# A contiguous copy of each unit's v as the moving operand of the sums over columns

## The chip, the cores and the metric

The kernel runs on one core of a Trainium2 chip. Its time is the device time of one execution in microseconds (us). A comparison of two kernels uses the median of several runs of each on the same chip. A core has five engines that work side by side: PE (TensorE, matrix products), DVE (VectorE), ACT (ScalarE), POOL (GpSimd) and SP (SyncE, which here only issues DMAs). Each goes through its own list of instructions in order and waits at semaphores for the others. Data is held in SBUF, 128 partitions wide; products are summed in PSUM, eight banks of 512 float32 numbers per partition.

## What is computed

A gated block of a sequence model on images: 8 images of 64 x 64 tokens with 96 channels. Each token's vector is divided by its root mean square, and projected to u and v of 288 channels each, with silu. v is then convolved, channel by channel, along the rows and along the columns of the image (`tno`), each with a kernel that a small network computes from the positions. The two results are added, multiplied by u, projected back to 96 channels, and added to x.

```python
xn = srms(x)
u = silu(xn @ u_w.T + u_b)
v = silu(xn @ v_w.T + v_b)
v = v.reshape(b, H, W, NH, HD).transpose(0, 3, 1, 2, 4)
out = (tno(v, -3, rpe2...) + tno(v, -2, rpe1...))
out = out.transpose(0, 2, 3, 1, 4).reshape(b, H, W, NH * HD)
return (u * out) @ o_w.T + o_b + x
```

The convolution of length 64 along one axis is a product with a 64 x 64 Toeplitz matrix for each channel, and two of them fit on 128 partitions.

## The kernel before

The images are worked on in two halves of four. v of one half lies whole in SBUF as `v`, 128 partitions x 128 columns m x 288 channels in float32 (147,456 bytes on each partition). The channel is the innermost index, so one channel's 128 columns lie 288 numbers, or 1152 bytes, apart. u goes to DRAM (`u_dram`) and comes back in tiles `u_in[0..3]` of 4608 bytes.

The program has five stages. **A**: the projection of half 0 in 32 steps, with the position networks beside its first ones. **C0**: the convolution of half 0. **B0**: 32 steps, each with the gate, output projection and store of half 0 and the projection of half 1. **C1**: the convolution of half 1. **B1**: gate, output projection and store of half 1.

A stage C treats the 288 channels as 36 units of 8. For unit n:

- DVE writes two Toeplitz tiles, `toepA` for the columns and `toepB` for the rows (line 749: each in two copies of 64 partitions x 512 numbers, from a `stage` tile that SP loads from `a_dram` by two DMAs, L271). In `stage` a channel's numbers lie 8 numbers (32 bytes) apart. Each Toeplitz tile has two buffers, `stage` three. The quarters that stay zero are written once by POOL (`zero`).
- PE does `along_columns(n)` (L951): 8 float32 products that sum over a column, with `toepA` held still and a channel of `v` moving. The profile has two records for each product, 16 a unit.
- PE does `transpose_v(n+1)` (L934): 8 transposes of v, evacuated by ACT to `vt` (L536).
- PE does `along_rows(n)` (L964): 8 products, again 16 records, that add into the same PSUM banks, with `vt` held still and `toepB` moving.
- ACT copies the sum back into `v` (L542, `evacuate_y`).

`toepA(n+2)` may be written when the columns of unit n are done (`columns_done`), `toepB(n+2)` when its rows are done (`conv_done`). The stage tile of unit n is loaded when both Toeplitz tiles of unit n-3 are written. In C0 DVE also computes the norms of half 1, in 8 groups of 4 steps: SP loads x into `x_n` (L236), POOL squares it (L403), DVE sums it (L655) and takes the root in 14 small operations (4 a unit). The next `x_n` is loaded when that sum is done. In C1 there is nothing of this.

The buffers in SBUF are placed by hand in one region above `v`; many share bytes at different times, and each such pair has a wait. `stage` shares bytes with `u_in`; `x_e` (the x that is added at the end) is loaded by L253 and stored by L259. Every order of instructions is written out by hand in the code.

Of the kernel before, what the change touches and what calls it, by code (L numbers as in the profile page):

```python
# [33 lines left out]
D = 288  # L34
RPE, LAYERS = 256, 3
EPS = 1e-8
P = 128
H = P // 2
# [18 lines left out]
def tno_kernel(nc, x, x_eT, u_wT, u_b, v_wT, v_b, o_wT, o_b, pos_w, pos_b, lwT, lb, out_wT, out_b, out):  # L57
# [7 lines left out]
    with ctx:  # L65
# [21 lines left out]
        XHL = [22528, 28160]  # L87
# [3 lines left out]
        u_out = place("u_out", [P, NB, D], V + 32256)  # L91
        g = place("g", [KE, 2, NCH, TOK], V + 36864, f32r)
        g1 = [place(f"g1{k}", [KE, 2, NCH, TOK], V + 26624 + 12288 * k, f32r) for k in range(2)]
        x_n = place("x_n", [P, CH * NB, E], V + 18432)
# [17 lines left out]
        r_pw = place("r_pw", [P, 2, 2, RC], V + 32256)  # L112
        r_lb = place("r_lb", [P, 2, LAYERS, RC], V + 32288)
# [8 lines left out]
        assert base + K + 8672 <= nc.sbuf_usable_end  # L122

# [41 lines left out]
        vt_transposed, vt_ready = sem("vt_transposed"), sem("vt_ready")  # L165
# [27 lines left out]
        def _(sp):  # L193
# [80 lines left out]
            def after_networks():  # L274
                store_a()
                sp.wait_ge(a_stored, 32)
                load_stage(0, 0)
                load_stage(0, 1)

            def phase_a(c, first, last):  # L280
                if c + 3 < CHUNKS:
                    load_x_all(c + 3)
                for r in range(CH):
                    store_u(0, CH * c + r, u_in[:, r % 2], ua_stored[r % 2])
# [5 lines left out]
            def phase_c(half):  # L290
                if half == 0:
                    sp.wait_ge(ua_stored[1], 16 * (STEPS // 2))
                    load_norms(0)
                load_stage(half, 2)
                for n in range(STAGES, UNITS):
                    load_stage(half, n)
                    if half == 0 and n % 4 == 2 and n // 4 < CHUNKS:
                        load_norms(n // 4)
                    if n == 24:
                        if half == 0:  # L300
                            sp.wait_ge(ua_stored[0], 16 * (STEPS // 2))
                            load_xa(0, 0)
                            load_xa(1, 1)
                        else:
                            sp.wait_ge(ub_stored, 16 * STEPS)
                        load_u(half, 0, 0)
                if half:
                    for k in range(2):
                        sp.wait_ge(o_stored[0][k], 16 * (STEPS // 2))
                else:  # L310
                    sp.wait_ge(norms_summed, 2 * CHUNKS)
                for k in range((2, CH)[half]):
                    load_xe(half, k, k)
                for k in (2, 3, 1):
                    n = UNITS - STAGES + (2, 3, 1).index(k)
# [749 lines left out]
```

## Time and profile before

| what | us |
|---|---|
| median of 3 runs | 985.4 (981.99 to 985.67) |
| the profiled execution | 985.56, of which the span of the trace is 983.8 |
| stage A | 0 to about 179 |
| stage C0 | about 179 to 404 |
| stage B0 | about 404 to 631 |
| stage C1 | about 631 to 859 |
| stage B1 | about 859 to 984 |
| PE busy | 928.7 (94%) |
| DVE busy | 522.7 (53%) |
| ACT busy | 445.2 (45%) |
| POOL busy | 280.6 (29%) |

The trace is one execution. All times in it are counted from its span's start, and 1.8 us of the execution lie outside the span. The busy shares are means over stages that have different limits. PE's granted clock was 0.987 of full speed over the run.

### The profile page before, as it was taken

The numbers are of one execution on the slowest core, as the hardware profiler recorded it, in microseconds if no ns is written. First come the engines' busy times: TensorE is split into PE (matmuls) and PEld (weight loads), VectorE is DVE, ScalarE is ACT, GpSimd is POOL, SyncE is SP. The second block draws the span as 40 slices with busy tenths as digits, with TensorE's granted clock in tenths as the row PEclk, the third lists the DMA queues.
The fourth block names the chain that finished last, engine by engine and source line by source line (L and its number), as shares of the span: only waits on it lengthen the run. The fifth ranks groups of instructions, "written<-read, shape, count | busy, mean of one in ns | idle before, by whom it ended". The sixth has DMA issues, their size and how long they took to land.

```text
span 983.8 us, 17099 instructions
## 1 busy us (share of the span) xinstructions
PE 928.7 (94%) x6124; PEld 855.6 (87%) x6124; DVE 522.7 (53%) x918; ACT 445.2 (45%) x658; POOL 280.6 (29%) x191
## 2 busy tenths in 40 slices
PE   1999689999999999899999999899999999999888
PEld 1998589899999999889898989799999999877665
DVE  7665342486777774344444444444444444277665
ACT  1665467433333333466666666433333333244333
POOL 4332222111111120345454545100000000187664
PEclk9999889999999999999999999899999999999999
DMA  8554643665556553287878777553333434277785
GB/s 200 159 177 153 115 165 145 169 138 121 118 118 159 118 118 107 70 252 254 251 253 251 256 249 249 165 128 86 87 86 86 111 86 110 80 226 249 242 250 188
DMA packets 128871, 160.95 MB, mean 164 GB/s; under 512 B 67174, under 2 KB 93994, under 8 KB 128810
## 3 DMA queue, kind: packets, MB, share of 16 engines
q1 hardware_dynamic: 128810, 160.12, 57.8%
q8 instruction: 40, 0.66, 0.3%
q14 instruction: 21, 0.17, 0.1%
HBM read 109.46 MB, written 50.63 MB: 163 GB/s over the span
## 4 chain that ended last, share of the span: by engine, by line
PE 83%; DMA 10%; DVE 2%; SPq 1%; issue 1%; POOL 1%; ACT 1%; POOLq 0%; ACTq 0%; DVEq 0%
PE ps L951 25%; PE ps L888 20%; PE ps L964 13%; PE ps L908 9%; PE ps L934 6%; DMA out<-x_e 6%; PE ps L898 6%; PE ps L879 3%; DMA u_dram<-u_in 1%; DMA stage<-a_dram 1%; DMA a_dram<-r_a 1%; POOL u_in L456 1%; DMA x_all<-in_x 1%; PE ps L862 1%; DMA u_in<-u_dram 1%
## 5 line engine op out<-in xcount | busy, mean ns | idle before, releaser
L951 PE MATMUL ps<-v,toepA 128*128 128x128 f32 x1152 | 264.8, 396 | 4.4 <-DVE toepA L749 4.4
L456 POOL TENSOR_TENSOR u_in<-u_in,v 128x1152 f32<-128x1152 f32 (+2 forms) x66 | 170.8, 2592 | 294.8 <-ACT v L542 263.0
L951 PEld LDWEIGHTS ps<-v,toepA 128*128 128x128 f32 x1152 | 230.1, 206 | 18.0 <-issue 3.3
L536 ACT COPY vt<-ps 128x1024 f32<-128x1024 f32 x72 | 72.9, 1013 | 244.3 <-PE ps L934 244.3
L749 DVE COPY toepA<-stage 64x512 f32<-64x512 f32 x144 | 106.0, 736 | 132.1 <-PE ps L951 114.3
L908 PE MATMUL ps<-g,wo 96*96 96x512 f32 (+1 forms) x576 | 151.8, 399 | 0.0
L790 DVE TENSOR_TENSOR g<-ps,g 96x512 fp32r<-96x512 f32 x192 | 123.0, 680 | 43.0 <-ACT g L516 43.0
L964 PE MATMUL ps<-toepB,vt 128*128 128x128 f32 x1152 | 140.5, 275 | 0.0
L702 DVE TENSOR_TENSOR xl<-ps,xh 96x512 fp32r<-96x512 f32 x64 | 43.9, 686 | 180.0 <-ACT xh L497 180.0
L964 PEld LDWEIGHTS ps<-toepB,vt 128*128 128x128 f32 x1152 | 134.9, 192 | 0.0
L516 ACT CAST g<-ps 96x512 fp32r<-96x512 f32 x192 | 102.4, 586 | 68.7 <-PE ps L898 68.7
L888 PE MATMUL ps<-wv,xh 97*128 97x288 f32 x512 | 119.8, 309 | 12.4 <-ACT u_in L502 12.0
L749 DVE COPY toepB<-stage 64x512 f32<-64x512 f32 x144 | 96.2, 668 | 57.0 <-PE ps L964 51.4
L888 PE MATMUL ps<-wu,xh 97*128 97x288 f32 x512 | 123.9, 307 | 2.4
L908 PEld LDWEIGHTS ps<-g,wo 96*96 96x96 f32 (+1 forms) x576 | 89.7, 162 | 27.1
L898 PE MATMUL ps<-ident,u_in 128*96 128x128 f32 x768 | 100.1, 273 | 11.0 <-POOL u_in L456 10.8
L898 PEld LDWEIGHTS ps<-ident,u_in 128*96 128x96 f32 x768 | 85.4, 126 | 20.8 <-POOL u_in L456 8.6
L542 ACT COPY v<-ps 128x1024 f32<-128x1024 f32 x72 | 72.9, 1012 | 59.7 <-PE ps L964 59.7
L502 ACT ACTIVATE v<-ps 128x576 f32 (+1 forms) x128 | 83.5, 652 | 35.8 <-PE ps L888 23.8
L888 PEld LDWEIGHTS ps<-wv,xh 97*128 97x128 f32 x512 | 88.0, 192 | 13.4 <-ACT u_in L502 12.3
L888 PEld LDWEIGHTS ps<-wu,xh 97*128 97x128 f32 x512 | 89.2, 190 | 11.2 <-issue 3.9
L934 PEld LDWEIGHTS ps<-ident,v 128*128 128x128 f32 x576 | 77.0, 191 | 3.2
(66 smaller groups left out, 830.1 us busy)
## 6 DMA issues: line engine op xcount, KB each, us to landing
stage<-a_dram SPq DMA_DIRECT2D x144, 256.0 KB, 4.2
u_in<-u_dram SPq DMA_DIRECT2D x64, 576.0 KB, 5.3
u_dram<-u_in SPq DMA_DIRECT2D x32, 576.0 KB, 2.8
u_dram<-u_out SPq DMA_DIRECT2D x32, 576.0 KB, 3.3
x_e<-in_x_eT SPq DMA_DIRECT2D x64, 192.0 KB, 3.9
out<-x_e SPq DMA_DIRECT2D x64, 192.0 KB, 3.5
x_all<-in_x SPq DMA_DIRECT2D x16, 384.0 KB, 5.4
x_n<-in_x SPq DMA_DIRECT2D x16, 384.0 KB, 6.0
```

The source lines that it names most:

```text
L456: return nc.gpsimd.tensor_tensor(out=tile, in0=tile, in1=v[:, bass.ds(t * NB, NB), start:end], op=ALU.mult)
L502: nc.scalar.activation(target, ps[:, b:b + 2, 0:D], ACT.Silu).then_inc(silu_done, 1)
L516: nc.scalar.copy(tile[0:E, 0, k], ps[0:E, bank]).then_inc(gh_ready, 1)
L536: nc.scalar.copy(vt[n % 2][:], ps[:, VT_BANK:VT_BANK + 2].rearrange("p b (c m) -> p (b c) m", m=P)).then_inc(vt_ready, 1)
L749: nc.vector.tensor_copy((toepA, toepB)[axis][n % 2][rows, :, rows], stage[n % STAGES][rows, axis].rearrange("p k c -> p c k")[:, :, ::-1]) ...
L790: nc.vector.tensor_tensor(out=tile[0:E, 1, k], in0=ps[0:E, bank], in1=tile[0:E, 0, k].bitcast(f32), op=ALU.subtract).then_inc(gl_ready, 1)
L888: last = nc.tensor.matmul(ps[:, n, 0:D], (xh, xl)[xp][r % 2][:, n * P:(n + 1) * P], w[:, wp], start=(k == 0), stop=(k == len(SPLIT) - 1))
L898: last = nc.tensor.transpose(columns[:, n // 2, n % 2], u_in[:, r % CH, n, k * E:(k + 1) * E], ident[:])
L908: last = nc.tensor.matmul(ps[0:E, bank], wo[0:rows, wp, k], tile[0:rows, gp, k], start=(k + s == 0), stop=(k == NCH - 1 and s == len(SPLIT ...
L934: last = nc.tensor.transpose(ps[:, VT_BANK + c // NB, (c % NB) * P:(c % NB + 1) * P], v[:, :, UNIT * n + c], ident[:])
L951: last = nc.tensor.matmul(ps[:, SET_BANK[n % 2] + c // NB, (c % NB) * P:(c % NB + 1) * P], toepA[n % 2][:, c], v[:, :, UNIT * n + c], star ...
L964: last = nc.tensor.matmul(ps[:, SET_BANK[n % 2] + c // NB, (c % NB) * P:(c % NB + 1) * P], vt[n % 2][:, c], toepB[n % 2][:, c], start=Fals ...
```

## The change

ACT makes a copy of unit n of v with the channel outermost, so that each channel's 128 columns lie side by side: `vc` (`by_channels`), two buffers. `along_columns` takes its moving operand from `vc` instead of `v`. PE waits for `vc_ready`; ACT waits, before it writes a buffer of `vc` again, until the columns of the unit that used it are done. In ACT's list of a unit the evacuation of the sum of unit n-1 now stands first, then the copy for unit n+1, then the evacuation of the transposes of unit n+1.

To make room, buffers move. `vc[0]` shares bytes with `u_in[3]`, `vc[1]` with `x_e`. `stage` takes the places of `u_in[0..2]`. In stage A the odd steps store u from `u_out`, the even ones from `u_in[2]`. `toepB[1]` shares bytes with `u_out`. From this follow new waits and a new order on SP, POOL and DVE: the stage tile of unit 2 is loaded before `x_n`; the sums of squares are taken at units 2, 6, ... and no longer at 0, 4, ...; u and x_e for the stage after are loaded in the last units of the convolution.

```diff
-        stage = [place(f"stage{k}", [P, 2, H, UNIT], V + U_BYTES * (2, 3, 1)[k]) for k in range(STAGES)]
+        stage = [place(f"stage{k}", [P, 2, H, UNIT], V + U_BYTES * k) for k in range(STAGES)]
-        toepB = [place(f"toepB{k}", [P, UNIT, P], V + (28160, 32256)[k]) for k in range(2)]
+        toepB = [place(f"toepB{k}", [P, UNIT, P], V + (32768, 28672)[k]) for k in range(2)]
+        vc = [place(f"vc{k}", [P, UNIT, P], V + (13824, 18432)[k]) for k in range(2)]
...
+            def by_channels(half, n):
+                if n == 0:
+                    act.wait_ge(silu_done, PAIRS * STEPS * (half + 1) - 2)
+                if n < 2 and half:
+                    if n == 0:
+                        act.wait_ge(y_transposed, NCH * STEPS)
+                    else:
+                        for k in range(2):
+                            act.wait_ge(o_stored[0][k], 16 * (STEPS // 2))
+                if n >= 2:
+                    act.wait_ge(columns_done, UNITS * half + n - 1)
+                nc.scalar.copy(vc[n % 2][:], v[:, :, UNIT * n:UNIT * n + UNIT].rearrange("p m c -> p c m")
+                     ).then_inc(vc_ready, 1)
...
+                by_channels(half, 0)
                 evacuate_vt(0)
                 for n in range(UNITS):
+                    if n:
+                        evacuate_y(n - 1)
                     if n + 1 < UNITS:
+                        by_channels(half, n + 1)
                         evacuate_vt(n + 1)
                     elif half == 0:
                         high_x(STEPS, 0)
-                    evacuate_y(n)
+                evacuate_y(UNITS - 1)
...
             def phase_c(half):
                 if half == 0:
+                    sp.wait_ge(ua_stored[0], 16 * (STEPS // 2))
+                    load_stage(0, 2)
                     sp.wait_ge(ua_stored[1], 16 * (STEPS // 2))
                     load_norms(0)
-                load_stage(half, 2)
...
+                    load_u(half, k, k)
+                sp.wait_ge(columns_done, UNITS * half + UNITS - 1)
+                load_u(half, 3, 3)
+                sp.wait_ge(columns_done, UNITS * half + UNITS)
                 for k in range((2, CH)[half]):
                     load_xe(half, k, k)
...
+                else:
+                    dve.wait_ge(ua_stored[1], 16 * (STEPS // 2))
                 toeplitz(1, 1)
-                    if half == 0 and n % 4 == 0 and n // 4 < CHUNKS:
+                    if half == 0 and n % 4 == 2 and n // 4 < CHUNKS:
...
                     pe.wait_ge(toepA_ready, 2 * (N + 1))
+                    pe.wait_ge(vc_ready, N + 1)
...
-                                                toepA[n % 2][:, c], v[:, :, UNIT * n + c],
+                                                toepA[n % 2][:, c], vc[n % 2][:, c],
```

In the following lists a number behind a name is the buffer, and a row says what the instruction writes and reads, and what it waits for. ACT, first units of stage C0, before:

```order
L536 COPY vt_76<-ps 128x1024 [waits vt_transposed]
L536 COPY vt_77<-ps 128x1024 [waits vt_transposed]
L542 COPY v<-ps 128x128x8 [waits conv_done]
L536 COPY vt_76<-ps 128x1024 [waits conv_done,vt_transposed]
L542 COPY v<-ps 128x128x8 [waits conv_done]
```

and after:

```order
L551 COPY vc_76<-v 128x1024 [waits silu_done]
L559 COPY vt_78<-ps 128x1024 [waits vt_transposed]
L551 COPY vc_77<-v 128x1024
L559 COPY vt_79<-ps 128x1024 [waits vt_transposed]
L565 COPY v<-ps 128x128x8 [waits conv_done]
L551 COPY vc_76<-v 128x1024 [waits columns_done]
L559 COPY vt_78<-ps 128x1024 [waits conv_done,vt_transposed]
```

Each unit has one copy more, in front of the copy that releases PE's next transposes; unit 0's own copy stands ahead of everything.

PE, the first two units of stage C0, after (before, the same rows read `ps<-v` and have no `vc_ready`):

```order
L963 MATMUL ps<-ident,v 128x128 [waits silu_done]
L963 MATMUL ps<-ident,v 128x128 x7
L981 MATMUL ps<-vc_76,toepA_72 128x128 [waits toepA_ready,vc_ready,toep_zeroed,silu_done]
L981 MATMUL ps<-vc_76,toepA_72 128x128 x7
L963 MATMUL ps<-ident,v 128x128 [waits vt_ready]
L963 MATMUL ps<-ident,v 128x128 x7
L994 MATMUL ps<-toepB_74,vt_78 128x128 [waits toepB_ready,vt_ready,toep_zeroed]
L994 MATMUL ps<-toepB_74,vt_78 128x128 x7
```

No instruction of PE has moved; the columns have a wait and another operand.

SP, the end of stage C1 and the start of B1, before:

```order
L271 DMA stage_71<-a_dram 64x2x512
L253 DMA x_e_57<-in_x_eT 96x2x256 [waits o_stored01,o_stored00]
L253 DMA x_e_57<-in_x_eT 96x2x256 x3
L243 DMA u_in<-u_dram 128x1152 [waits toepB_ready,toepA_ready] x3
L243 DMA u_in<-u_dram 128x1152 [waits y_transposed] x2
```

and after:

```order
L277 DMA stage_71<-a_dram 64x2x512
L249 DMA u_in<-u_dram 128x1152 [waits ub_stored,toepB_ready,toepA_ready]
L249 DMA u_in<-u_dram 128x1152 [waits toepB_ready,toepA_ready] x2
L249 DMA u_in<-u_dram 128x1152 [waits columns_done]
L259 DMA x_e_57<-in_x_eT 96x2x256 [waits columns_done]
L259 DMA x_e_57<-in_x_eT 96x2x256 x3
L249 DMA u_in<-u_dram 128x1152 [waits y_transposed] x2
```

The first u tile was loaded earlier, at unit 24. Now all four u tiles and the x_e tiles come at the end, the last of them behind the final columns.

## Rows read from the trace of the kernel before

**Rows 1.** The page, part 4: the chain that ended last, by engine and line.

```profile
PE 83%; DMA 10%; DVE 2%; SPq 1%; issue 1%; POOL 1%; ACT 1%; POOLq 0%; ACTq 0%; DVEq 0%
PE ps L951 25%; PE ps L888 20%; PE ps L964 13%; PE ps L908 9%; PE ps L934 6%; DMA out<-x_e 6%; PE ps L898 6%; PE ps L879 3%; DMA u_dram<-u_in 1%; DMA stage<-a_dram 1%; DMA a_dram<-r_a 1%; POOL u_in L456 1%; DMA x_all<-in_x 1%; PE ps L862 1%
```

**Rows 2.** Busy by stretch: PE, PEld, DVE, ACT, POOL (count each), clock, DMA, GB/s.

```profile
202.00:398.00 196.00, 196.00 (x1272) 188.72 (x1271) 133.67 (x240) 63.80 (x63) 24.90 (x10) 1.00 0.54 125
...
649.00:858.90 209.90, 209.84 (x1355) 201.79 (x1353) 86.67 (x130) 67.86 (x68) 2.40 (x1) 1.00 0.37 92
```

**Rows 3.** Timeline, one unit of stage C1: start, duration, engine, line, operation.

```profile
655.16 3.38 PEld L951 LDWEIGHTS ps<-v,toepA 128*128 128x128 f32 x16
...
655.47 1.01 ACT L542 COPY v<-ps 128x1024 f32<-128x1024 f32 x1 [0.77 <-PE ps L964]
655.47 1.35 DVE L749 COPY toepB<-stage 64x512 f32<-64x512 f32 x2 [1.30 <-PE ps L964]
658.55 1.08 PEld L934 LDWEIGHTS ps<-ident,v 128*128 128x128 f32 x8
...
658.98 1.40 DVE L749 COPY toepA<-stage 64x512 f32<-64x512 f32 x2 [2.16 <-PE ps L951]
659.55 1.87 PEld L964 LDWEIGHTS ps<-toepB,vt 128*128 128x128 f32 x16
...
661.33 3.38 PEld L951 LDWEIGHTS ps<-v,toepA 128*128 128x128 f32 x16
```

**Rows 4.** The page, part 5: groups by line, out<-in, count, busy, mean, idle before.

```profile
L951 PE MATMUL ps<-v,toepA 128*128 128x128 f32 x1152 | 264.8, 396 | 4.4 <-DVE toepA L749 4.4
...
L536 ACT COPY vt<-ps 128x1024 f32<-128x1024 f32 x72 | 72.9, 1013 | 244.3 <-PE ps L934 244.3
```

**Rows 5.** Timeline, the start of stage C0.

```profile
179.24 0.65 ACT L502 ACTIVATE u_in<-ps 128x576 f32<-128x576 f32 x1 [0.17 <-PE ps L888]
...
179.77 3.38 PEld L951 LDWEIGHTS ps<-v,toepA 128*128 128x128 f32 x16
...
183.44 1.32 SPq L236 DMA_DIRECT2D x_n<-in_x  x2
...
191.86 1.75 DVE L749 COPY toepA<-stage 64x512 f32<-64x512 f32 x2 [8.21 <-DMA stage<-a_dram]
...
193.66 3.36 PEld L951 LDWEIGHTS ps<-v,toepA 128*128 128x128 f32 x16 [1.43 <-DVE toepA L749]
```

**Rows 6.** Timeline, the start of stage C1.

```profile
635.62 3.56 PEld L951 LDWEIGHTS ps<-v,toepA 128*128 128x128 f32 x16 [3.29 <-issue]
...
636.24 0.33 SPq L259 DMA_DIRECT2D out<-x_e  x1
...
642.78 3.38 PEld L951 LDWEIGHTS ps<-v,toepA 128*128 128x128 f32 x16
```

**Rows 7.** Timeline of DVE and POOL in stage C0, around squares of x_n.

```profile
254.63 2.61 DVE L605 TENSOR_SCALAR n_tmp<-n_tmp 128x16 f32<-128x16 f32 x1
...
260.81 1.75 DVE L655 TENSOR_REDUCE n_tmp<-x_n 128x16 f32<-128x1536 f32 x1
...
277.96 3.83 DVE L749 COPY toepA<-stage 64x512 f32<-64x512 f32 x2 [2.18 <-PE ps L951]
278.39 2.90 POOL L403 TENSOR_TENSOR x_n<-x_n 128x1536 f32<-128x1536 f32 x1 [21.18 <-DMA x_n<-in_x]
```

**Rows 8.** The page, part 6: DMAs, count, KB each, us from issue to landing.

```profile
stage<-a_dram SPq DMA_DIRECT2D x144, 256.0 KB, 4.2
...
out<-x_e SPq DMA_DIRECT2D x64, 192.0 KB, 3.5
...
x_n<-in_x SPq DMA_DIRECT2D x16, 384.0 KB, 6.0
```

**Rows 9.** The chain in order of time, stage B1: start, duration, what.

```profile
897.68 3.87 DMA out<-x_e
...
901.57 0.32 SPq L253
```

More of the change, by code:

```diff
@@ L111, in tno_kernel @@
         wo_raw = place("wo_raw", [KE, NCH, E], V + 55552)
-        r_pw = place("r_pw", [P, 2, 2, RC], V + 32256)
-        r_lb = place("r_lb", [P, 2, LAYERS, RC], V + 32288)
+        r_pw = place("r_pw", [P, 2, 2, RC], V + 18432)
+        r_lb = place("r_lb", [P, 2, LAYERS, RC], V + 18464)
         K = V + 56704
@@ L122, in tno_kernel, with u_tile @@
         assert base + K + 8672 <= nc.sbuf_usable_end
+        def u_tile(half, r):
+            return u_out if half or r % 2 else u_in[:, 2]
         ps = ctx.enter_context(nc.psum_tensor("ps", [P, 8, 512], f32))
@@ L276, in after_networks @@
                 sp.wait_ge(a_stored, 32)
-                load_stage(0, 0)
-                load_stage(0, 1)
+                for n in range(2):
+                    load_stage(0, n)
             def phase_a(c, first, last):
@@ L338, in body @@
                         if t == STEPS - 1:
-                            for n in range(2):
-                                sp.wait_ge(y_transposed, NCH * (t + n))
+                            sp.wait_ge(y_transposed, NCH * t)
+                            for n in range(STAGES):
                                 load_stage(1, n)
@@ L443, in _ @@
             zero(toepA[1], 2)
-            zero(toepB[1], 4)
             pool.wait_ge(projected, PAIRS * STEPS)
-            zero(toepB[0], 6)
+            zero(toepB[0], 4)
+            pool.wait_ge(ua_stored[1], 16 * (STEPS // 2))
+            zero(toepB[1], 6)
             for j in range(CHUNKS):
@@ L527, in phase_a @@
                     for pair in range(2):
-                        silu_u(0, t, pair, u_in[:, r % 2], ua_stored[r % 2], 32 * c + 16 * (r // 2))
+                        silu_u(0, t, pair, u_tile(0, r), ua_stored[r % 2], 16 * (2 * c + r // 2) if isinstance(c, int) else 32 * c + 16 * (r // 2))
             chunks(act, phase_a)
+            def by_channels(half, n):
[11 more added lines that the diff above has]
+                     ).then_inc(vc_ready, 1)
             def phase_c(half):
@@ L769, in phase_c @@
                         toeplitz(0, n + 2)
-                    if half == 0 and n % 4 == 0 and n // 4 < CHUNKS:
+                    if half == 0 and n % 4 == 2 and n // 4 < CHUNKS:
                         sum_a1(n // 4)
                         pieces = iter(norms_a1(n // 4))
-                    if half == 0:
+                    if half == 0 and n >= 2:
                         run(itertools.islice(pieces, 4))
@@ L938, in zeroed_for @@
                 def zeroed_for(n):
-                    return ((2, 8), (4, 6)) if half == 0 else ((2, 10), (12, 14))
+                    return ((2, 6), (4, 8)) if half == 0 else ((2, 10), (12, 14))
                 def along_columns(n):
```

41 lines of the change are left out of this document (18 added, 23 removed).

## The prediction, made before the changed kernel ran

> **What bounds the kernel now.** I read the chain that ended last first: PE holds 83% of it, and the sums over columns, L951, are its largest line with 25%, against 13% for the sums over rows, L964 [rows 1]. Then the stretches: in the steady part of both convolution stages PE is busy for the whole stretch at a granted clock of 1.00 (2.4 GHz) [rows 2]. So in these stages PE sets the time, and what is taken from PE there comes off the end, as long as no other engine takes its place. L951 sat idle for 4.4 us in all its 1152 records [rows 4].
>
> Then one unit [rows 3]. It lasts from 655.16 to 661.33, 6.17 us: columns from 655.16 to 658.55 (3.39 us), transposes to 659.55 (1.00), rows to the next unit's columns at 661.33 (1.78). Columns and rows are the same work, 8 float32 products of 128 x 128 by 128 columns in 16 records, yet the columns take 1.9 times as long. What differs is the moving operand. That of the rows, `toepB`, lies side by side; that of the columns steps through `v` by 1152 bytes. The transposes read the same stepped `v` as the operand that is held still and take 1.00 us for 8, so a stepped weight load is not what is slow. I take the stepped moving read for the cause.
>
> The Trainium skill has a rule for this (Advanced Engine Details and Errata, SBUF Cachelines): float32 reads that go to a different 16-byte line each time pay a penalty, since at least two hits on a line are needed to hide the memory's latency. The trace agrees for PE, 3.39 against 1.78 us. The same rule speaks against the new copy, whose source is stepped in the same way; by it the copy takes about twice an ACT copy, some 2.0 us, and by the nearest row 1.0. The sum below is the same by both.
>
> **The change part by part.**
>
> *Columns.* 72 units, each shorter by 3.39 - 1.78 = 1.61 us [rows 3]. I take 1.60: **-115.2 us**. PE's unit becomes 3.39 - 1.60 + 1.00 + 1.78 = about 4.58 us. With no part of it gained the price is 0; more than this has no row that speaks for it, since the rows' product is the same shape.
>
> *The copy on ACT.* 72 copies of 128 x 1024, not in the trace. The two ACT copies of a unit take 1.01 us each for the same size; one of them writes `v` with the same step [rows 3, 4]. From above: PE gets 128 stepped columns in 3.39/16 = 0.21 us, 1.7 ns each. If ACT can read only as fast as that, 1024 numbers take 1.7 us, and 1.9 with what an instruction costs besides. DVE copies 512 numbers that step by 32 bytes in 0.70 us [rows 3], 1.3 ns each at most, so a step over lines isn't dear for a slower reader. I take 1.05 us, nearest to the ACT rows, and keep 1.0 to 1.9. ACT then does 2.02 + 1.05 = 3.1 us a unit (3.9 at the upper bound) of 4.58. In order: `evacuate_y(n-1)` starts when the rows of n-1 end, that is when the columns of n begin; it and the copy end 2.1 to 3.0 us later, and the transposes for `vt(n+1)` are ready at 2.8. PE wants `vc` at 4.58 and `vt` at 4.58 + 1.8. Both have over 1.5 us in hand, so the copy costs nothing in the steady part. It would cost from 4.58 - 2.1 = 2.5 us a copy on.
>
> *The first unit of C0.* Its copy is behind ACT's last silu, which ends at 179.24 + 0.65 = 179.89; PE's columns started at 179.77 [rows 5]. They now start at about 179.9 + 1.05 + 0.1 = 181.0: **+1.2**. Next to go: DVE waited 8.21 us for the stage tile of unit 2, which was queued behind `x_n`, and PE waited 1.43 for DVE [rows 5]. The tile now goes out before `x_n`, when the even u tiles are stored. What is late next is `toepA(3)`: its stage tile now stands where that of unit 2 stood, behind `x_n`, so it lands at about 191.9. It is copied by 193.6; PE wants it at 181.0 + 3 x 4.58 = 194.7. **-1.4**. `toepB(1)` waits for the last u store, on DVE and on POOL (the zeros), until about 183.4; the rows of unit 1 want it at 188.4. Nothing.
>
> *The start of C1.* The copy of unit 1 waits on ACT for the last store of half 0's output, which is issued at 636.24 and lands 3.5 us later [rows 6, 8]; behind it in ACT's list stands the `vt` of unit 1. `vc` is then ready at about 641. PE's columns of unit 0 start at 635.62 as before, and those of unit 1 could start about 1.6 us before the 642.78 of now, at 641.2 [rows 6]. I count 0.4 (0 to 2): **+0.4**.
>
> *Ends of C0 and C1.* u tiles are loaded from unit 33 on, some 14 us before the end, instead of in part from unit 24; four loads of 576 KB fit, and POOL's first gate needs one. The x_e tiles (768 KB at the end of C1) go out when the last columns are done, but the first is wanted some 8 us later. In C0 the third `xa` load is now behind two x_e loads on SP and may hold POOL back by 1 us. In B1 the chain ends in a ring of stores, waits and loads of x_e, 3.87 + 0.32 us a step [rows 9], so that stage is held by transfers in its later part, and what SP issues later at its start may come back there. I count **+0.5** for B0 and **+0.5** for B1 (-1 to +4 together).
>
> *DVE in C0.* This is the closest cover. In the stretch 202 to 398 DVE is busy for 133.67 us, in 240 instructions [rows 2]. That is 196/6.18 = 31.7 units, so 4.22 us and 7.6 instructions a unit; with about 0.04 us between instructions it is 4.5 us of the new 4.58. It has three large pieces: the Toeplitz copies (1.40 + 1.35), the sum over x_n (1.75 every fourth unit, with 4 small operations a unit), and one DVE operation in four units that sits out POOL's squaring: a small operation takes 2.61 us and a pair of copies 3.83 instead of 1.40 while POOL works on x_n [rows 7]. Two buffers let DVE be late by some 6 us before PE waits (`toepA(n+2)` is free to write 7.4 us before it is used and takes 1.4), so a mean of 4.5 fits. I count **+1** for single misses. In C1, without norms, DVE has 2.75 us a unit. Nothing.
>
> *Transfers in C.* A stage tile is freed when `toepB(n-3)` is written, about 11.0 - 1.4 = 9.6 us before `toepA(n)` can be started; two DMA issues (1.3) and 4.2 us to land make 5.5, and 8 behind an `x_n` load (6.0 to land) [rows 8]. They fit. `x_n` itself: from one sum to the next there are 18.3 us, and issue, landing and squaring need 1.3 + 6.0 + 2.9 = 10.2 [rows 7, 8].
>
> The moved tiles of stage A and the waits that come with them keep two u tiles in turn, as before: nothing.
>
> **Sum:** -115.2 + 1.2 - 1.4 + 0.4 + 1.0 + 1.0 = -113.0. On the profiled execution, 985.56: 872.6. The median of the runs, 985.4, stands 0.2 lower. **Forecast 872.5 us.**
>
> **The rivals.**
>
> *DVE becomes the bound in C0.* For it: 4.5 of 4.58 us is a thin margin, and the denser DVE works, the surer each squaring on POOL hits it, or hits it twice; against it: the lateness that the buffers allow. If each squaring cost another 2.5 us (a second blocked operation of the size of rows 7), four units would take 18.0 + 2.5 = 20.5 against 18.3, and eight groups +18 us: 890. A quarter of that is 877.
>
> *ACT becomes the bound.* If the stepped copy cost 3.5 us, a unit would be 3.5 + 2.1 = 5.6 us, +1.0 on 72: 945. No row shows an engine so slow on a step. **Slower than before** it would be from the point where ACT's unit passes 6.18 us, that is where a copy takes over 4.1 us, 4 ns a number; at 4.5 us, 6.6 a unit: 985 + 0.4 x 72 = 1014.
>
> *The step isn't the cause,* and PE needs 3.39 us for the columns from `vc` too. For it: the rows add to a bank and the columns open it, which no row separates from the step. Against it: the transposes open their banks too and are fast. Then only the edges are left: 985.6 + 1.2 - 1.4 + 1.4 = about 987.
>
> **How the numbers follow.** Forecast as told, 0.72. DVE binds C0 in part or whole (876 to 892), 0.15. ACT binds, but faster than before (890 to 980), 0.03. The step isn't the cause, 0.05. Slower by the copy, 0.02. Better than the sum, because the edges cost nothing (866 to 870), 0.03. The range goes from 867 (edges and misses at nothing, and B1 not held back) to 884 (half of the first rival): it leaves out about 0.05 below and 0.13 above. A measurement of this kernel can tell about 0.5% from no change, 5 us. Faster by more: 0.93; within: 0.05; slower: 0.02.
>
> **What would show it.** In the changed profile, columns of unit n last about 1.8 us from first weight load to the transposes, and a unit 4.6; PE busy falls by some 115 us and stays at 1.0 of each stretch in C; the ACT copy takes 1.0 to 1.1 us (1.9 by the other bound) and nobody waits for it but PE's unit 0 and perhaps unit 1 of C1; DVE in C0 has hardly any idle time, and PE's wait for `toepA` and `toepB` is a few us in total. The prediction is wrong if units in C0 take over 4.7 us while those of C1 take 4.6 (DVE), if both take as long as ACT's three copies (ACT), if the columns still take 3.4 us (the step), or if stage B1 is longer than its 125 us by more than a few.

## The result and the profile after

The changed kernel takes 864.58 us (median of 4 runs, 863.47 to 867.52) against 984.25 us for the kernel before (4 runs): the ratio is 0.8791, with a 95% interval from 0.8761 to 0.8821. The profiled executions took 865.25 and 985.56 us, with spans of 863.5 and 983.8. The direction was right and the gain was larger than forecast: 119.7 us against 112.9 forecast, and 864.6 lies 2.4 us below the range's lower end of 867. So the question is not why the change works but where 7 us more came from.

The page of the changed kernel, parts 1 and 4 (busy time, then the chain that ended last, by engine and line; L981 is the sums over columns, L994 over rows, L963 the transposes):

```profile
PE 806.7 (93%) x6124; PEld 748.3 (87%) x6124; DVE 526.6 (61%) x918; ACT 601.3 (70%) x730; POOL 282.5 (33%) x191
...
PE 76%; DMA 14%; DVE 4%; SPq 2%; issue 1%; POOL 1%; ACT 1%; POOLq 0%; DVEq 0%; ACTq 0%
PE ps L917 23%; PE ps L981 14%; PE ps L994 13%; PE ps L937 9%; DMA out<-x_e 8%; PE ps L963 7%; PE ps L927 6%; PE ps L908 3%; DMA stage<-a_dram 2%; POOL u_in L463 1%; DMA u_in<-u_dram 1%; DMA a_dram<-r_a 1%; DVE toepA L776 1%; DMA u_dram<-u_
```

The columns held 25% of the chain [rows 1] and now hold 14%, next to 13% for the rows: the same work has come to the same price. PE is busy for 122 us less, about the whole gain. ACT is busy for 156 us more.

One unit of C1 in the timeline of the changed kernel, to be held against [rows 3]:

```profile
649.83 1.87 PEld L981 LDWEIGHTS ps<-vc,toepA 128*128 128x128 f32 x16
...
650.14 1.01 ACT L565 COPY v<-ps 128x1024 f32<-128x1024 f32 x1 [0.23 <-PE ps L994]
...
651.05 2.40 ACT L551 COPY vc<-v 128x1024 f32<-128x1024 f32 x1
...
651.61 0.97 PEld L963 LDWEIGHTS ps<-ident,v 128*128 128x128 f32 x8
651.72 1.06 PE L963 MATMUL ps<-ident,v 128*128 128x128 f32 x8
...
652.51 1.87 PEld L994 LDWEIGHTS ps<-toepB,vt 128*128 128x128 f32 x16
...
653.31 1.06 ACT L559 COPY vt<-ps 128x1024 f32<-128x1024 f32 x1
654.30 1.87 PEld L981 LDWEIGHTS ps<-vc,toepA 128*128 128x128 f32 x16
```

From one first weight load to the next: columns 1.78 us (649.83 to 651.61), as forecast; transposes 0.90 (to 652.51), where I had left them at 1.00; rows 1.79; the unit 4.47 instead of 4.58. The copy takes 2.40 us, over the 1.9 that I took for its upper bound, and nobody waits for it here. ACT has 0.23 us of idle time left.

The busy time by stretch, steady part of C0 and of C1 (PE, PEld, DVE, ACT, POOL, clock, DMA share, GB/s), to be held against [rows 2]:

```profile
202.00:338.00 136.00, 135.56 (x1208) 135.00 (x1207) 129.31 (x237) 126.86 (x91) 23.20 (x10) 1.00 0.71 162
590.00:735.00 145.00, 145.00 (x1301) 145.00 (x1300) 87.33 (x128) 137.00 (x98) 2.50 (x1) 1.00 0.49 121
```

DVE is busy 95% of the stretch in C0, ACT 93 to 94% in both; in these stretches PE waits nowhere in C1 and 0.44 us in C0.

By stages, from the first transposes of a convolution to the first product of the next stage. Over a whole stage a unit takes 6.19 us in the mean before and 4.47 after; the fifth column is what 36 such units give.

| stage | before, us | after, us | difference | 36 x (4.47 - 6.19) | left over |
|---|---|---|---|---|---|
| A | 178.85 | 178.34 | -0.5 | | -0.5 |
| C0 | 224.90 | 165.52 | -59.4 | -61.9 | +2.5 |
| B0 | 227.49 | 227.45 | 0.0 | | 0.0 |
| C1 | 229.29 | 168.92 | -60.4 | -61.9 | +1.5 |
| B1 | 123.27 | 123.27 | 0.0 | | 0.0 |

The units alone gave 123.8 us where I had counted 115.2: this one term is 8.6 us too small. The edges cost 4.0 us in the convolution stages, where I had 2.2 for all edges and misses together. This is one execution of each kernel, and what is left over is of the size of the scatter: a second profiled execution of the changed kernel (after_again) has 164.8 us for C0 and 169.8 for C1. B1 scatters most, from 122.0 to 127.1 us over the executions below, though none of them changes it.

### The profile page after: what moved, and what is told of

The parts are those of the page before. It is cut to its first block, busy times and chain, and to the rows that moved or that the text cites. A ratio compares the mean times of both kernels' runs of the same rounds, so it can differ in the third digit from the quotient of the medians.

```text
span 863.5 us, 17178 instructions
## 1 busy us (share of the span) xinstructions
PE 806.7 (93%) x6124; PEld 748.3 (87%) x6124; DVE 526.6 (61%) x918; ACT 601.3 (70%) x730; POOL 282.5 (33%) x191
## 4 chain that ended last, share of the span: by engine, by line
PE 76%; DMA 14%; DVE 4%; SPq 2%; issue 1%; POOL 1%; ACT 1%; POOLq 0%; DVEq 0%; ACTq 0%
PE ps L917 23%; PE ps L981 14%; PE ps L994 13%; PE ps L937 9%; DMA out<-x_e 8%; PE ps L963 7%; PE ps L927 6%; PE ps L908 3%; DMA stage<-a_dram 2%; POOL u_in L463 1%; DMA u_in<-u_dram 1%; DMA a_dram<-r_a 1%; DVE toepA L776 1%; DMA u_dram<-u_in 1%; SPq L259 1%
## 5 line engine op out<-in xcount | busy, mean ns | idle before, releaser
L551 ACT COPY vc<-v 128x1024 f32<-128x1024 f32 x72 | 170.4, 2366 | 6.1 <-DMA out<-x_e 6.1
L981 PE MATMUL ps<-vc,toepA 128*128 128x128 f32 x1152 | 142.8, 278 | 6.8 <-DVE toepA L776 4.0
L981 PEld LDWEIGHTS ps<-vc,toepA 128*128 128x128 f32 x1152 | 136.0, 194 | 8.0 <-issue 6.3
L994 PE MATMUL ps<-toepB,vt 128*128 128x128 f32 x1152 | 140.4, 275 | 0.0
L994 PEld LDWEIGHTS ps<-toepB,vt 128*128 128x128 f32 x1152 | 134.6, 192 | 0.0
L776 DVE COPY toepA<-stage 64x512 f32<-64x512 f32 x144 | 112.9, 784 | 29.4 <-PE ps L981 14.8
L509 ACT ACTIVATE u_out<-ps 128x576 f32<-128x576 f32 x96 | 62.5, 652 | 60.8 <-PE ps L917 58.1
```

Of the source, the lines that this page charges most:

```text
L509: nc.scalar.activation(target, ps[:, b:b + 2, 0:D], ACT.Silu).then_inc(silu_done, 1)
L551: nc.scalar.copy(vc[n % 2][:], v[:, :, UNIT * n:UNIT * n + UNIT].rearrange("p m c -> p c m")).then_inc(vc_ready, 1)
L776: nc.vector.tensor_copy((toepA, toepB)[axis][n % 2][rows, :, rows], stage[n % STAGES][rows, axis].rearrange("p k c -> p c k")[:, :, ::-1]) ...
L981: last = nc.tensor.matmul(ps[:, SET_BANK[n % 2] + c // NB, (c % NB) * P:(c % NB + 1) * P], toepA[n % 2][:, c], vc[n % 2][:, c], start=(c % ...
L994: last = nc.tensor.matmul(ps[:, SET_BANK[n % 2] + c // NB, (c % NB) * P:(c % NB + 1) * P], vt[n % 2][:, c], toepB[n % 2][:, c], start=Fals ...
```

## The experiments

Two questions were taken to the chip. First, what exactly was slow: the width of the step, the crossing of a line in memory, or the copy's and the transposes' own reads. Second, what the other engines have in hand. Kernels that were executed once are given with the kernel before on the same chip beside them; it differed by up to 4 us from chip to chip (984.3 to 988.4), so I read units and stages from their traces first and whole times second.

### A step of 16 bytes

```diff
-        vc = [place(f"vc{k}", [P, UNIT, P], ...
+        vc = [place(f"vc{k}", [P, UNIT // 4, P, 4], ...
-                nc.scalar.copy(vc[n % 2][:], v[...].rearrange("p m c -> p c m")
+                nc.scalar.copy(vc[n % 2][:], v[...].rearrange("p m (g c) -> p g m c", c=4)
-                                                toepA[n % 2][:, c], vc[n % 2][:, c],
+                                                toepA[n % 2][:, c], vc[n % 2][:, c // 4, :, c % 4],
```

> The changed kernel, but vc holds the unit in two groups of 4 channels, so that PE's moving operand steps by 16 bytes, not 4. Theory A (each float32 that is read from another 16-byte line costs PE double): columns last 3.39 us as in the kernel before and the transposes behind them 1.00, a unit 6.18, the whole about 865 + 72 x 1.72 = 988 us; ACT's copy, which now reads runs of 4 neighbours from v, falls from 2.4 to about 1.0 us. Rival B (only the wide step of 1152 bytes is slow): columns 1.78 us, about 864 us.

It took 993.8 us, the kernel before 988.4. Timeline, one unit of C1:

```profile
703.23 3.48 PEld L981 LDWEIGHTS ps<-vc,toepA 128*128 128x128 f32 x16
...
704.45 1.05 ACT L551 COPY vc<-v 128x1024 f32<-128x1024 f32 x1
...
706.73 1.11 PEld L963 LDWEIGHTS ps<-ident,v 128*128 128x128 f32 x8
...
707.75 1.87 PEld L994 LDWEIGHTS ps<-toepB,vt 128*128 128x128 f32 x16
...
709.54 2.57 PEld L981 LDWEIGHTS ps<-vc,toepA 128*128 128x128 f32 x12
```

Columns 3.50 us, transposes behind them 1.02, a unit 6.31. So a step of 16 bytes costs all that the step of 1152 cost, and 0.11 us a unit more (3.50 against 3.39); why it is dearer stays open. Rival B, that only wide steps are slow, is out. ACT's copy, which reads runs of four here, fell to 1.05 us as expected.

### A step of 8 bytes

The same with groups of 2.

> The changed kernel, but vc holds the unit in four groups of 2 channels: PE's moving operand steps by 8 bytes, two reads to a line of 16 bytes, and ACT reads v in pairs. Theory A: columns 1.78 us as from the contiguous copy, unit 4.47; the copy 1.0 to 1.2 us instead of 2.4, so that the two places where PE waits for it at the start of the convolution stages shrink by about 1 us each: 862 to 864 us. Rival C (any step other than 4 bytes is slow): columns 3.39 us, about 988 us.

867.7 us, with 988.4 for the kernel before. One unit of C1, and the copy's group over the whole run (busy, mean ns):

```profile
651.20 1.89 PEld L981 LDWEIGHTS ps<-vc,toepA 128*128 128x128 f32 x16
...
652.42 1.12 ACT L551 COPY vc<-v 128x1024 f32<-128x1024 f32 x1
...
653.02 0.96 PEld L963 LDWEIGHTS ps<-ident,v 128*128 128x128 f32 x8
653.13 1.04 PE L963 MATMUL ps<-ident,v 128*128 128x128 f32 x8
```

```profile
L551 ACT COPY vc<-v 128x1024 f32<-128x1024 f32 x72 | 81.7, 1135 | 8.3 <-DMA out<-x_e 8.3
```

Columns 1.82 us, unit 4.48. Two reads to 16 bytes are nearly as good as four, for PE (1.82 against 1.78) and for ACT (1.12 us against 1.05 from runs of four). Rival C, any step but 4 bytes, is out. So the three layouts together bear out the rule that the prediction took from the Trainium skill (Advanced Engine Details and Errata, SBUF Cachelines), for PE and for ACT, at the number of hits per line that it names.

The total missed its 862 to 864 us. Of the two waits, the one at the start of C0 shrank (PE's weight loads idle for 1.17 us, 2.04 in the changed kernel), the one at unit 1 of C1 did not (1.17 against 1.10), since it hangs on a store. Against that, a unit of C1 takes 4.50 us in the mean instead of 4.47, 1.1 us in the stage.

### The transposes ahead of the columns

```diff
                 for n in range(UNITS):
-                    along_columns(n)
                     if n + 1 < UNITS:
                         transpose_v(n + 1)
                     elif half == 0:
                         transpose_x(STEPS, 0)
+                    along_columns(n)
```

> The kernel before, with PE's transposes for unit n+1 ahead of the columns of unit n instead of behind them. Theory D (the 0.10 us that the transposes lost with the change is the tail of the last stepped product, which lay in their time): the transposes last 0.90 us, and what now stands behind the columns, the rows, 1.89 instead of 1.78; unit and whole as before, within 2 us of 985. Rival E (the transposes themselves got faster because vc relieves v): they stay at 1.00 us.

983.2 us, the kernel before 988.4. One unit of C1:

```profile
703.47 0.96 PEld L934 LDWEIGHTS ps<-ident,v 128*128 128x128 f32 x8
...
704.35 3.38 PEld L951 LDWEIGHTS ps<-v,toepA 128*128 128x128 f32 x16
...
707.74 1.99 PEld L964 LDWEIGHTS ps<-toepB,vt 128*128 128x128 f32 x16
707.96 1.96 PE L964 MATMUL ps<-toepB,vt 128*128 128x128 f32 x16
...
709.65 0.97 PEld L934 LDWEIGHTS ps<-ident,v 128*128 128x128 f32 x8
```

The transposes last 0.88 us here, with v as it was, and the rows 1.91 instead of 1.78. The extra 0.1 us moved to whatever follows the columns. It is the tail of the last stepped product: the weight load of the next group is counted from its start, and its first product waits for the last stepped one. Here the rows' first product starts 0.22 us behind its weight load. In the changed kernel the transposes' first product starts 0.11 us behind (651.61, 651.72); in the kernel before it stood 0.22 us behind the load at 658.55 of [rows 3]:

```profile
658.77 1.05 PE L934 MATMUL ps<-ident,v 128*128 128x128 f32 x8
```

Theory D holds, E falls. The total of this one execution, 5 us below the kernel before, is outside the 2 that I allowed; its units are 6.18 us as before. Against the profiled execution of the kernel before the span is 2.4 us shorter, and 1.9 of it stand in A and B1, which this edit does not touch; C0 is the same and C1 0.5 less. So I make nothing of it.

### All of the change, but PE reads v

```diff
-                                                toepA[n % 2][:, c], vc[n % 2][:, c],
+                                                toepA[n % 2][:, c], v[:, :, UNIT * n + c],
```

> The changed kernel with all its waits, buffers and copies, but PE's columns read v again and not vc. Theory (the whole gain is the contiguous operand; placement, order and the copy give nothing): columns 3.39 us, unit 6.18 to 6.2, the whole 984 to 988 us. Rival F (part of the gain comes from the new placement, such as the earlier stage tile): below 982 us. It also shows whether ACT's copy lasts 2.4 us beside stepped products too.

987.9 us, the kernel before 988.4. A unit takes 6.20 us again (700.67 to 706.87), the columns 3.40 and the transposes 1.01. Placement, order and copies alone give nothing that can be measured. The copy lasts 1.95 us in this run, beside products whose moving operand steps through `v`:

```profile
L551 ACT COPY vc<-v 128x1024 f32<-128x1024 f32 x72 | 141.4, 1964 | 7.1 <-DMA out<-x_e 7.1
```

### What the copy's 2.4 us are made of

Two runs. In the first the copy reads 128 contiguous numbers eight times:

```diff
-                nc.scalar.copy(vc[n % 2][:], v[...].rearrange("p m c -> p c m")
+                nc.scalar.copy(vc[n % 2][:], ident[:].unsqueeze(1).to_broadcast([P, UNIT, P])
```

> The changed kernel, but ACT fills vc from 128 contiguous numbers read eight times (the identity), so that the columns are summed over the wrong data; size and target of the copy are the same. Theory A for ACT (the copy's 2.0 to 2.4 us come from the stepped source): it lasts 1.0 to 1.1 us. Rival I (a copy from SBUF to SBUF is slow as such): it stays above 1.9 us. The whole 862 to 865 us either way, since the copy is off PE's path but for two waits at the starts.

In the second the copy is as it was, and PE's transposes for units 1 to 33 take their held operand from a contiguous tile:

```diff
-                                                   v[:, :, UNIT * n + c], ident[:])
+                                                   vc[(n - 1) % 2][:, c] if 0 < n < 34 else v[:, :, UNIT * n + c], ident[:])
```

> The changed kernel, but PE's transposes for units 1 to 33 read a contiguous tile (the vc of the unit before) in place of v, so the rows are summed over the wrong unit. ACT's copy lasts 1.96 us where PE is idle and 2.39 in the steady part. Theory K (the difference is the conflict with PE's transposes, which step through v at the same time): the copy falls to about 2.0 us. Rival L (it comes from any PE or DVE traffic): it stays at 2.3 to 2.4. The transposes themselves stay at 0.90 us, since the held operand's step cost nothing before; if they fall, their weight load was slowed by the step.

In the first the columns are summed over the wrong data, in the second the rows over the wrong unit; the amount of work is the same. They took 864.0 and 864.9 us, the kernel before 986.2. The copy in the first, then the copy and the transposes' weight loads in the second (count, busy, mean ns):

```profile
L551 ACT COPY vc<-ident 128x1024 f32<-128x1024 f32 x72 | 75.6, 1050 | 7.9 <-DMA out<-x_e 7.9
```

```profile
L551 ACT COPY vc<-v 128x1024 f32<-128x1024 f32 x72 | 148.4, 2062 | 5.8 <-DMA out<-x_e 5.8
...
L963 PEld LDWEIGHTS ps<-ident,vc 128*128 128x128 f32 x528 | 61.5, 143 | 0.0
```

A contiguous source: 1.05 us. The stepped source: 1.96 us where nothing interferes. The remaining 0.3 to 0.4 us go when PE's transposes no longer take their held operand from `v` during the copy: theory K. In the same way the copy lasted 1.95 us beside the slower columns of the run before, where it was over before the transposes began. So it is not PE's stepped reading of `v` as such that lengthens the copy, for the moving operand did so there, but the stepped weight loads. Whether they must read the same tile for it is not separated; a copy from a contiguous source beside them stays at 1.05 us. In the transposes PE's weight load does notice the step, 192 ns against 143, but a transposing block takes 0.90 us with it and 0.88 without: the load is hidden behind the products. (A record of 192 ns alone is no sign of a step: the loads of `toepA` and `vt`, which are contiguous, show it too.) That is why the transposes of the kernel before told me nothing about the step.

### How much ACT has in hand

Four runs. One takes the copy nearly away (from unit 2 on it has 1 of 8 channels, and leaves the other seven out):

> The changed kernel, but from unit 2 on ACT copies only one of the 8 channels, so the other seven are summed over old data. Theory (PE alone sets the unit): unit 4.47 as with the full copy, the whole 862 to 865 us. Rival J (the copy takes something from PE in the steady part, by lateness or by SBUF reads): the unit gets shorter, the whole below 860 us.

864.5 us, unit 4.47: PE alone sets it. One cuts the copy into four instructions of 2 channels:

> The changed kernel with ACT's copy cut into four instructions of 2 channels each. ACT now has 1.01 + 2.39 + 1.01 = 4.41 us of work in a unit of 4.47. Theory G (ACT is within 0.1 us of taking PE's place): each further instruction costs ACT some 0.15 to 0.2 us, so ACT has about 4.95 us a unit, the unit follows it to about 4.95, and the whole to about 865 + 70 x 0.48 = 899 us. Rival H (ACT has time in hand, as I predicted, because its copies overlap or buffers carry it): below 870 us.

869.3 us, the kernel before 986.2. I had expected 899, and the unit is still 4.47 us. The four took 2.58 us from the first's start to the last's end: back to back they overlap, and three more instructions cost 0.2 us together, not 0.5 to 0.6. The total is 4 to 5 us above the others of this chip, and 4 of them stand in B1 (127.1 us instead of 123.3). This edit doesn't touch B1, and B1 scatters by as much from execution to execution: 122.0 in t_first, 125.0 in t_contig, 126.2 in early_step8. The next adds an instruction of its own kind:

```diff
+                if n >= 4:
+                    wait(act, extra, 32 * half + n - 4)
+                    nc.scalar.copy(ps[:, 7, 0:256]..., v[:, :, UNIT * n:UNIT * n + 2]...).then_inc(extra, 1)
```

> The changed kernel with one more copy on ACT for each unit from the fifth on: 128 x 256 numbers from v to an unused PSUM bank, about 0.55 to 0.7 us. From the timeline ACT's three copies fill 4.23 of the 4.47 us of a unit (they overlap by 0.1 us each). Theory G' (ACT has 0.24 us in hand and no more): the unit becomes 4.23 + 0.6 = 4.8 us, 64 units give +23 us, about 888. Rival H (ACT is far from binding): under 870 us.

866.2 us against an expected 888, the second miss. In its timeline ACT has no idle time left, and PE does not wait:

```profile
650.45 1.87 PEld L986 LDWEIGHTS ps<-vc,toepA 128*128 128x128 f32 x16
...
650.80 1.06 ACT L570 COPY v<-ps 128x1024 f32<-128x1024 f32 x1
651.70 0.69 ACT L554 COPY ps<-v 128x256 f32<-128x256 f32 x1
...
652.24 2.28 ACT L556 COPY vc<-v 128x1024 f32<-128x1024 f32 x1
...
654.37 1.06 ACT L564 COPY vt<-ps 128x1024 f32<-128x1024 f32 x1
654.92 1.87 PEld L986 LDWEIGHTS ps<-vc,toepA 128*128 128x128 f32 x16
```

From start to start ACT's four instructions take 0.90, 0.54, 2.13 and 0.90 us, together 4.47. So the idle time of 0.23 us understated what ACT has in hand, for two reasons. In the changed kernel 1.30 us passed from the start of the copy to `vt` (653.31) to the next unit's first copy; back to back it is 0.90, as here, because the instructions overlap. That makes 0.40 us of room. And the copy to `vc` took 2.26 us from its start to the next instruction's, here 2.13; with that the 0.54 us are covered. Why it got shorter is only in part known: the transposes (652.24 to 653.21) still lie almost wholly beside it. The last doubles the addition:

> As act_extra, but the additional copy has 128 x 512 numbers (4 channels, 1.1 to 1.2 us). With 128 x 256 ACT had no idle time left and a unit still took 4.47 us, its instructions starting 0.90, 0.54, 2.13 and 0.90 us after one another. Theory G'' (ACT was then exactly full): the unit becomes 4.47 + 0.45 to 0.5 = 4.95 us and the whole 865 + 64 x 0.47 = about 895 us. Rival H (something else gives way again): under 870 us.

893.3 us, the kernel before 984.5. Now it binds:

```profile
672.80 1.86 PEld L986 LDWEIGHTS ps<-vc,toepA 128*128 128x128 f32 x16 [0.40 <-issue]
...
674.22 1.49 ACT L554 COPY ps<-v 128x512 f32<-128x512 f32 x1
...
675.43 2.24 ACT L556 COPY vc<-v 128x1024 f32<-128x1024 f32 x1
...
677.33 1.25 ACT L564 COPY vt<-ps 128x1024 f32<-128x1024 f32 x1
...
677.74 1.86 PEld L986 LDWEIGHTS ps<-vc,toepA 128*128 128x128 f32 x16 [0.40 <-issue]
```

A unit of 4.94 us, as long as ACT's four (1.21 + 1.90 + 0.91 + 0.90 = 4.92). Here the copy starts at 675.43, when the last transposes end, and takes 1.90 us from start to start, as theory K wants. With the two evacuations at 1.81 us, ACT takes over where copy and addition pass 4.47 - 1.81 = 2.66 us: 2.67 cost nothing, 3.11 cost 0.47 a unit.

### A version that beats both

PE's largest single wait left in the convolution stages is at the start of C1. It waits 3.0 us for the first Toeplitz tile, whose stage tile is loaded late, and then runs the columns of unit 0 at half clock. Timeline and stretch of the changed kernel, and the same stretch of the kernel before:

```profile
575.59 3.48 PEld L981 LDWEIGHTS ps<-vc,toepA 128*128 128x128 f32 x16 [3.20 <-issue]
```

```profile
575.50:579.00 3.50, 3.38 (x16) 3.41 (x17) 3.04 (x5) 0.00 (x0) 0.00 (x0) 0.51 1.02 315
```

```profile
635.50:639.10 3.60, 3.45 (x16) 3.48 (x17) 3.48 (x5) 0.00 (x0) 1.30 (x2) 0.50 0.48 163
```

The contiguous columns take 3.4 us at 1.2 GHz; the stepped ones took 3.47 us at 1.2 GHz and 3.39 at 2.4. The step holds PE to what half the clock does, so the columns of this unit gained only 0.1 us from the change. Its transposes gained more: the low clock lasted through them in the kernel before (1.68 us to the rows, 0.50 of full speed) and ended with the columns in the changed one (0.92 us, 0.97):

```profile
639.09 1.70 PEld L934 LDWEIGHTS ps<-ident,v 128*128 128x128 f32 x8
```

```profile
578.96 1.00 PEld L963 LDWEIGHTS ps<-ident,v 128*128 128x128 f32 x8
```

The stage tiles of the first two units can be loaded one step of B0 earlier, when their u tiles are free:

```diff
-                        if t == STEPS - 1:
-                            sp.wait_ge(y_transposed, NCH * t)
-                            for n in range(STAGES):
-                                load_stage(1, n)
+                        if t == STEPS - 2:
+                            sp.wait_ge(y_transposed, NCH * t)
+                            for n in range(2):
+                                load_stage(1, n)
+                        if t == STEPS - 1:
+                            sp.wait_ge(y_transposed, NCH * t)
+                            load_stage(1, 2)
```

Three kernels were timed on one chip, five executions each: the changed kernel again, this edit alone, and this edit with the copy in groups of 2 channels.

> The changed kernel once more, as the partner of the two runs below on the same chip: 863 to 868 us.

> The changed kernel, but the stage tiles of the first two units of C1 are loaded one step of B0 earlier (7 us), as soon as u_in[0] and u_in[1] are free. PE sat idle for 3.2 us there, and then ran the columns of unit 0 at half clock, in 3.5 us instead of 1.8, with a granted clock of 0.51. Theory M (the idle time causes the low clock): with a gap of about 1.2 us, which ACT's first copy leaves, the clock stays up, and both go: 2.0 + 1.7 us, about 861 us. Rival N (the low clock comes with the change of stage, whatever the gap): only 2 us go. Rival O (what is won at the start is waited for at unit 1, whose copy waits for the last store of half 0's output, which lands at 580.7): under 1 us goes in the end.

> The same with vc in four groups of 2 channels, so that ACT's copy lasts 1.1 instead of 2.0 to 2.4 us. Against the last one PE waits 1 us less at the start of C0 and 1 us less at the start of C1: about 2 us less if the store does not hold unit 1 back, 1 us less if it does.

| kernel | median, us | ratio to the kernel before, 95% interval |
|---|---|---|
| changed | 865.99 | 0.8787 [0.8765, 0.8809] |
| stage tiles earlier | 862.27 | 0.8761 [0.8737, 0.8785] |
| the same, copy in groups of 2 | 860.65 | 0.8738 [0.8718, 0.8758] |

The last is 5.3 us below the changed kernel, and the two intervals do not meet. That the middle one is faster than the changed one is likely, but its interval overlaps with both neighbours. In the profiled executions C1 lasted 169.8, 166.9 and 165.6 us, so rival O (the gain is waited for at unit 1) is out. The first columns of C1 in the timelines of the middle and the last, each followed by the stretch:

```profile
573.30 3.43 PEld L983 LDWEIGHTS ps<-vc,toepA 128*128 128x128 f32 x16 [2.33 <-issue]
```

```profile
573.30:576.60 3.30, 3.27 (x15) 3.30 (x16) 2.31 (x4) 1.68 (x2) 1.25 (x2) 0.50 0.97 200
```

```profile
573.63 1.89 PEld L983 LDWEIGHTS ps<-vc,toepA 128*128 128x128 f32 x16 [1.51 <-issue]
```

```profile
573.60:575.50 1.90, 1.84 (x16) 1.87 (x17) 1.78 (x3) 0.83 (x1) 0.00 (x0) 1.00 0.99 386
```

In the middle kernel PE now waits for ACT's copy instead of the Toeplitz tile; its weight loads are idle for 2.33 us. ACT's last silu waits 2.77 us for a store of u, which was issued right behind the early loads and landed 6.4 us later, where the page's median for these stores is 3.3. The clock fell to half again. In the last the copy is 1 us shorter, the gap 1.51 us, and the granted clock stayed full: 1.82 us for the columns. So the low clock is no fixed part of the change of stage (N), as far as this one execution shows, and the first edit by itself did not make the gap short, which I had expected at 1.2 us.

That the length of the idle time is the cause (M) is not shown. The start of C0 speaks against so simple a rule. There the weight loads had been idle for 2.0 us in eight executions; over the next columns the granted clock was 1.00 in four of them (after, after_again, act_extra, act_extra4) and 0.66 to 0.83 in the others (early_stage, copy_small, t_contig, read_v), and in step16 it was 0.85 after 1.11 us. In early_stage it looks like this:

```profile
179.80:182.50 2.70, 2.65 (x16) 2.68 (x17) 1.82 (x3) 2.69 (x2) 1.39 (x2) 0.66 1.05 174
```

Its unit 0 of C0 took 6.09 us instead of 4.47. In the last kernel the gap at C0 was 1.16 us and the clock 1.00, so part of what the last gains on the middle one may stand there.

## Why the prediction was wrong, point by point

- **The bound and the cause.** PE bound both stages, and the stepped moving operand was the cause. The result shows it, and read_v and the three layouts show it apart from everything else; of the rivals "the step isn't the cause" and "slower" nothing came.
- **The step that failed: the columns' term.** I read 3.39 - 1.78 = 1.61 us from the first weight load of one group to that of the next and wrote that more than this had no row that speaks for it. It had: the transposes behind the columns took 1.00 us in [rows 3], and part of that was the tail of the last stepped product; their first product stood 0.22 us behind its weight load. So the term put at 1.60 us a unit, -115.2 us, measured 1.72 a unit, -123.8 us, with about 0.11 of the difference in the transposes and 0.01 in my rounding of 1.61. 0.12 x 72 = 8.6 us is more than the whole miss. t_first shows the tail moving to the rows when these come next. The mechanism was right; this term was mis-sized, and the lower end of the range had been set from the edges alone, with no bound of its own for the largest term.
- **The edges together.** Forecast +2.2, measured +3.5 (4.0 in the convolution stages, -0.5 in A, which is within the scatter). That these are near each other is partly luck: +1.0 for B0 and B1 never came, and the starts of C0 and C1 cost more than forecast.
- **The copy on ACT.** Forecast 1.05 us with 1.0 to 1.9; measured 1.96 alone and 2.4 in place. The rows that I took it from (copies that read PSUM and write v with the step) say nothing on a stepped read; the bound from PE's rate was the right row and was nearly met, but could not hold a conflict with PE's stepped weight loads. The row of DVE (0.70 us for 512 numbers, 1.4 ns each and not 1.3) has no contiguous partner, so it could not show that a step isn't dear for a slower reader; for ACT it doubles the copy. The 2.0 us that the prediction worked out by the rule of the Trainium skill (Advanced Engine Details and Errata, SBUF Cachelines) came near the 1.96; the section gives no factor, and the two came from PE's rows. It changed nothing in the sum, since the place was right: nobody waits for it in the steady part. The point from which ACT would bind, "2.5 us a copy", is 2.66.
- **The first unit of C0.** Forecast +1.2. PE waited 1.87 us for the copy, which lasted 1.96 us there instead of 1.05 (the first line below). The 1.43 us wait at unit 2 went, as forecast. What was late next was named rightly, `toepA(3)`; it was not ready in time as I had counted but 0.5 us late:

```profile
181.39 2.02 PE L981 MATMUL ps<-vc,toepA 128*128 128x128 f32 x16 [1.87 <-ACT vc L551]
...
193.45 2.00 DVE L776 COPY toepA<-stage 64x512 f32<-64x512 f32 x2 [3.77 <-DMA stage<-a_dram]
...
195.50 1.86 PEld L981 LDWEIGHTS ps<-vc,toepA 128*128 128x128 f32 x16 [0.67 <-DVE toepA L776]
```

  PE wanted it at about 194.8, as forecast (194.7). The load landed 1.5 us later than I took it for, and the copy, at the side of POOL's squaring (191.54 to 194.30), took 2.00 us instead of 1.7.
- **The start of C1.** Forecast +0.4. PE waited 0.93 us at unit 1 for the copy that waits for the last store, as told, and unit 0's columns gained 0.1 us at half clock where 1.6 were counted, which I had not seen. Its transposes and rows gave back some 0.9, since the low clock ended sooner. Together 1.5 over the units:

```profile
582.88 2.02 PE L981 MATMUL ps<-vc,toepA 128*128 128x128 f32 x16 [0.93 <-ACT vc L551]
```

- **DVE in C0.** Right: 95% busy, and one squaring in four units lengthens one DVE operation, as forecast (3.75 us for the two copies at 205.81 and at 223.75). The first rival had 0.15 and did not come; PE idled 0.44 us in 136.
- **B0 and B1.** Forecast +1.0 together, measured 0.0: both stages have the length that they had. At the start of B0 POOL did wait 1.07 us for `xa`, and the stage was no longer for it. In B1 the ring of stores and loads of x_e still sets the later part.

## What to carry to other kernels

An operand that PE streams should have two float32 neighbours in each 16 bytes; a step of 8 bytes is enough for all but 0.03 us a unit, and makes the copy that prepares it twice as fast as a full reordering. When a pipelined engine's slow group is costed from the start of one group to the start of the next, look at the group behind it as well: its tail lies there, and with 72 repeats it was the whole error. Idle time of an engine can understate what it can take, because instructions back to back overlap and because their length depends on what they run beside; adding work until it binds gave the true figure.

## What the runs showed of the hardware

- Stepped float32 operands of PE, 8 products of 128 x 128 by 128 columns: 1.78 us at a step of 4 bytes, 1.82 at 8, 3.50 at 16, 3.39 at 1152; at half clock the contiguous one takes 3.4 and the one with 1152 bytes 3.47, hardly more than its 3.39 at full clock.
- The group behind eight stepped products (1152 bytes) takes 0.11 us longer, whether it is the transposes or the rows (1.00 against 0.90, 1.91 against 1.78).
- ACT copying 128 x 1024 float32 within SBUF: 1.05 us from a contiguous source or from runs of 4, 1.12 from runs of 2, 1.96 from single numbers, also beside products whose moving operand steps through the same tile, and 2.4 while PE loads stepped weights from it (2.06 when those loads are contiguous).
- PE's weight load of 128 x 128 float32 in the transposes: 143 ns contiguous, 192 ns stepped, with 0.02 us of effect on a block of eight. In the products a contiguous load is recorded with 192 ns as well.
- PE's granted clock over the first columns of C1 was 1.00 after 1.51 us without a weight load (one execution), 0.65 after 1.87 (t_first), and 0.50 to 0.51 after 2.33 and 3.20 us. At the start of C0, after 2.0 us, it was 1.00 in four executions and 0.66 to 0.83 in four others.
- Stage B1, whose instructions are the same in all the variants of the changed kernel, took 122.8 to 127.1 us in their profiled executions.
